# Issuing four scatter DMAs ahead of a bias addition on GpSimd in two of the sixteen blocks of a cross-attention and mixture-of-experts kernel

## The reference

```python
x = x + _L0_xattn_ref(_layernorm(x), ctx_1024, Wq, bq, Wk, bk, Wv, bv, Wo, bo)
x = x + _L0_ffn_ref(_layernorm(x), W_experts, b_experts, W_router, b_router)

# inside _L0_ffn_ref, shortened
router_weights = softmax(einsum('bsd,ed->bse', x, W_router) + b_router)
topk_w, topk_idx = top_k(router_weights, 2)        # all other weights become 0
expert_out = einsum('bsd,eod->bseo', x, W_experts) + b_experts
return einsum('bseo,bse->bso', expert_out, router_weights)
```

## Time and profile before

| | |
|---|---|
| median of 3 runs | 1247.7 us (1247.05 to 1251.27) |
| the profiled execution | 1251.27 us; its span 1249.6 us |
| TensorE busy | 1173.5 us, 94% of the span |
| VectorE, ScalarE, GpSimd busy | 869.7, 712.5, 762.5 us (70, 57, 61%) |
| mean granted TensorE clock | 0.977 |

### The profile page before, as it was taken

The page is one execution under the profiler, slowest core; times in us unless marked ns, Lnnn a source line. Parts: engine busy times, 40 slices in busy tenths (PEclk is TensorE's granted clock), DMA queues, the critical chain, the costliest instruction groups (busy, mean ns, idle before and its releaser), DMA issues. The chain is left out here.

```text
span 1249.6 us, 35422 instructions
## 1 busy us (share of the span) xinstructions
PE 1173.5 (94%) x10864; PEld 708.9 (57%) x10865; DVE 869.7 (70%) x1931; ACT 712.5 (57%) x1040; POOL 762.5 (61%) x996
## 2 busy tenths in 40 slices
PE   7977999999999999999999988799999999999995
PEld 4454666666666666666666655444545555455552
DVE  3665798899889889988987886555545555455553
ACT  4327757866976886696687557243333334333432
POOL 5004347777877877787787678765554545445444
PEclk9978999999999999999999998799999999999998
DMA  9764445755866675586557548889999999988885
GB/s 243 225 180 123 130 139 162 227 183 179 256 185 204 197 224 188 184 253 185 200 178 204 168 148 339 305 189 202 204 184 184 191 183 177 179 168 160 156 165 106
DMA packets 136312, 239.18 MB, mean 191 GB/s; under 512 B 19463, under 2 KB 50183, under 8 KB 135047
## 3 DMA queue, kind: packets, MB, share of 16 engines
q1 hardware_dynamic: 103271, 161.24, 43.6%
q0 software_dynamic: 29808, 67.73, 26.7%
q10 hardware_dynamic: 3120, 8.68, 2.0%
HBM read 112.00 MB, written 101.40 MB: 171 GB/s over the span
## 5 line engine op out<-in xcount | busy, mean ns | idle before, releaser
L1904 PE MATMUL S<-we_s,wq_s 128*128 x1620 | 371.8, 379 | 11.7 <-DVE att L1882 8.3
L1832 POOL DMA_INDIRECT out<-xn,to x135 | 208.9, 1547 | 198.6 <-DMA out<-xn,to 90.1
L1904 PEld LDWEIGHTS S<-we_s,wq_s 128*128 128x128 f16 x1620 | 156.6, 98 | 177.3 <-issue 16.2
L1166 POOL TENSOR_TENSOR we_s<-P_s,we_s 128x1024 f16<-128x1024 f32 x96 | 204.7, 2135 | 72.8 <-ACT we_s L932 71.6
L1843 ACT ACTIVATE wq_s<-PVp 128x512 f16<-128x512 f32 x137 | 81.6, 597 | 249.7 <-PE PVp L1894 249.7
L980 DVE TENSOR_REDUCE mx_sb<-S 128x6 f32<-128x924 f32 x160 | 171.1, 1110 | 10.5 <-PE S L726 8.9
L746 PE MATMUL W<-wo_s,aT_hi 128*128 128x512 f16 x512 | 165.3, 385 | 2.7 <-DVE aT_lo L958 1.4
L708 PE MATMUL W<-we_s,wq_s 128*128 128x512 f16 x512 | 160.9, 386 | 3.7 <-DVE xnT_lo L958 3.6
L1882 DVE SCALAR_TENSOR_TENSOR att<-S,be_s 128x512 f32<-128x512 f32 x135 | 93.4, 692 | 98.8 <-PE S L1904 98.2
L1262 POOL DMA_INDIRECT dispatched<-xn,idx x112 | 114.9, 1026 | 26.7 <-issue 24.0
L1860 DVE TENSOR_TENSOR wq_s<-PVp,wq_s 128x512 f16<-128x512 f32 x137 | 94.6, 691 | 35.1 <-ACT wq_s L1843 35.1
(11 more groups left out here) (204 smaller groups left out, 1948.3 us busy)
## 6 DMA issues: line engine op xcount, KB each, us to landing
P_s<-dispatched SPq DMA_DIRECT2D x139, 260.5 KB, 3.8
we_s<-we_s SPq DMA_DIRECT2D x186, 128.0 KB
be_s<-in_x SPq DMA_DIRECT2D x16, 1024.0 KB, 8.9
xR_s<-in_x SPq DMA_DIRECT2D x16, 1024.0 KB, 8.2
out<-xR_s SPq DMA_DIRECT2D x16, 1024.0 KB, 5.9
wst<-in_weT SPq DMA_DIRECT2D x16, 512.0 KB, 5.7
we_scratch<-wsp SPq DMA_DIRECT2D x16, 512.0 KB, 9.2
Kst<-k_scratch SPq DMA_DIRECT2D x16, 480.0 KB, 9.0
```

The lines of the kernel that those rows point to most:

```text
L1166: e.tensor_tensor(Pst[1][:, r:r + 2, :], exps(n), Pst[0][:, r:r + 2, :], ALU.subtract).then_inc(pldp, 1)
L1832: e.indirect_dma_start(out, bass.IndirectOffsetOnAxis(ap=to[u][:, :], axis=0), yw[u % YW], None, bounds_check=N - 1, oob_is_err=False, com ...
L1904: m = e.matmul(Yp[:, u % 2, :], gT[u % 2][xp][:, k, :], we_s[:, bass.ds(n * WN + (wp * KC + k) * D, D)], start=(c == 0), stop=(c == 11))
```

## The change

In `pool_slot` the call of `pool_SC(e, bm1)` now stands before `pool_BX(e, b, 3)`; it stood behind it. The condition is unchanged (`early1` is true for blocks up to 11 and in the loop, so `pool_SC` is issued only for `bm1` = 12 and 13).

```diff
         if early1:
             pool_S1(e, bm1, 1)
+        elif on_bm1 and bm1.here(NB - 3):
+            pool_SC(e, bm1)
         if on_b:
             pool_BX(e, b, 3)
         if early1:
             pool_S1(e, bm1, 2)
-        elif on_bm1 and bm1.here(NB - 3):
-            pool_SC(e, bm1)
```

## The result

| | before | after |
|---|---|---|
| median, us | 1247.75 (7 runs, 1247.05 to 1252.38) | 1257.72 (7 runs, 1250.99 to 1262.6) |
| profiled execution, us | 1251.27 | 1254.19 |
| its span, us | 1249.6 | 1252.4 |
| first expert tile, us from the start | 809.84 | 813.20 |

The change makes the kernel slower: the ratio is 1.0058 with a 95% interval of 1.0037 to 1.0080, which is +7.2 us. The medians lie 10.0 us apart. The ratio is smaller because it also takes in seven further runs of the changed kernel, 1254.94 to 1256.96 us: the mean of its 14 runs is 1256.4 us, that of the kernel before 1249.1 us. The forecast was +3.6 us, 1251.3 us, with a range up to 1254.3; the median of 1257.7 us lies above the range, and so does the mean.

What follows compares the result with a forecast made beforehand. TensorE is busy 377.15 of 399 us in the second stage; the change can only shift its start, through GpSimd's order in block 14's slot. 0 + 4.5 - 0.9 = +3.6 us on 1247.7: 1251.3 us, range 1248.3 to 1254.3.

Steps and rivals of the forecast that it cites:

- The path: From GpSimd in block 14's slot to the first expert tile: L992 4.5 us late, L1019 and tile 3.6 us late.
- the hand-over to the first scatter: Block 14's slot, ScalarE's L620 to GpSimd: the first scatter starts 0.23 us behind L620's end, at 779.78.
- the 0.9 us at L597: Block 14's slot: L597 no longer waits for the scatters, so 0.9 us of the delay is won back.
- Block 13's slot: The addition is ready 0.4 us before L992 needs it, covered by VectorE's row of maxima; cost 0.
- First rival: At the kernel's end, waits set by earlier DMA traffic absorb up to half of 3.6 us, say 1249 us; chance 0.13.
- none of the four forecasts: The forecast shift of 2.5 to 4.6 us (chance 0.68), absorbed (0.13), larger (0.14) and faster (0.05).
- Second rival: TensorE's clock returns one group later in block 15's projection, adding 2.6 us: +6.2, 1253.9 us; chance 0.14.
- Third rival: On GpSimd the addition runs beside the scatters, L992 is not late, 0.9 us gained, 1246.8 us; chance 0.05.

Runs made afterwards that it cites:

- e10: Kernel before with only block 13's four scatters ahead of block 14's addition, block 13's slot as before; chip 5: 1.0036 of the kernel before.
- e9: Kernel before with only block 12's four scatters ahead of block 13's addition, block 14's slot as before; chip 5: 1.0003 of the kernel before.
- e11: Kernel before with the fourth of block 13's first scatters moved behind the norm in block 14's slot; chip 5: 0.9996 of the kernel before.
- e2: Kernel before with only block 12's four scatters ahead of block 13's addition, block 14's slot as before; chip 7: 0.9994 of the kernel before.
- e18: Kernel before with loads of experts 3 to 7 cut to a sixteenth and the experts' index at most 2; chip 10: 0.9989 of the kernel before.
- e1: The changed kernel again, no edit; chip 7: 0.9987 of the kernel before.
- e3: Kernel before with only block 13's four scatters ahead of block 14's addition, block 13's slot as before; chip 7: 0.9988 of the kernel before.
- e14: Changed kernel with 22 matmuls that nothing reads in TensorE's pause ahead of block 14's L847; chip 4: 0.9997 of the kernel before.
- e16: The changed kernel again, no edit; chip 4: 0.9981 of the kernel before.
- e4: Kernel before with the fourth of block 13's first scatters moved behind the norm in block 14's slot; chip 7: 1.0001 of the kernel before.
- e17: The kernel before again, no edit; chip 10: 1.0006 of the kernel before.
- e5: The kernel before again, no edit; chip 2: 0.9994 of the kernel before.
- e8: The changed kernel again, no edit; chip 2: 1.0043 of the kernel before.
- e7: Changed kernel with loads of experts 3 to 7 cut to a sixteenth and the experts' index at most 2; chip 2: 1.0037 of the kernel before.
- e12: Kernel before, GpSimd's order untouched, with 12 unread statistics instructions on VectorE ahead of block 14's L992 for group 3; chip 5: 1.0037 of the kernel before.
- e13: Changed kernel with two of block 14's slot's four scatters ahead of the addition and two behind; chip 4: 0.9972 of the kernel before.

## Why the prediction failed

**The path: right.** L1248 late, L992, the norm, L597, L1195, L1019, block 15's projection, the first tile: each of them moved, in this order, and the times forecast for the first profile (addition 784.73, L992 786.11, L597 789.35, L1019 792.7, tile 813.4) stand within 0.21 us of what it shows (784.55, 785.92, 789.14, 792.52, 813.20). Part of that is luck: the execution was 0.81 us early, and a term was too small by about as much.

**The step that failed: the hand-over to the first scatter, a term of the sum that was too small by 0.7 us.** The working took 0.23 us from ScalarE to GpSimd, from a tensor instruction. The first scatter started 779.65 - 778.74 = 0.91 us behind L620. In the earlier trace rows the scatter had 0.16 us ahead of it, but it could have begun 1.2 us earlier for ScalarE's part (L620 ended at 779.55), and what it needs before its start could pass beside the addition; that this is the reason is argued, and only the two times are measured. With 0.91 in its place the sum is 0.91 + 4.87 + 0.03 + 1.27 + 0.10 = 7.18 us from L620's end to L992, as measured, and L992 is 5.14 us late, not 4.5. Less the 0.9 us at L597 it is +4.2 us, the ruler's number. That alone would have given 1251.9 us, inside the range. e10 shows the same hand-over on chip 5: L620 ends at 777.74, the scatter starts at 778.66.

**Block 13's slot, 0: right.** L992 stays behind L985 here, with the addition done 1.27 us before it (the working had 0.6 us), and e9 measures 1.0003.

**The 0.9 us at L597: right.** L597 starts 0.22 us behind L582; e11 has the gain alone, 0.7 to 0.9 us.

**First rival, absorbed.** Not on the chips on which the kernel takes 1247 us: from the first tile to the end of the span it is 439.8 us before and 439.2 after. On chips 4 and 7 nothing is lost, but not by what the rival named. In three of the four traces of the slower chips that leave L992 early and have no fillers, the same stretch has extra waits that those with the late L992 don't have: e2 and e18 lose 4.7 us to them and read 26.2 on the ruler, where e1, e3, e14 and e16 read 25.7 to 25.8; e4 loses 3.6; e17 loses nothing. It is a case that none of the four forecasts held; the first trace has no such gap.

**Second rival, the clock.** Half-speed groups come in kernels of either order: 6.7 us in the first trace of before and in e5, with no such pause, and 4.56 us in e10 and e16 behind it. **Third rival, scatters beside the engine.** Disproved: the addition starts 0.03 us behind the end of the fourth scatter's row, and L992 waits for it. The four rows hold the engine up to their right edge. The Trainium skill, page "Perfetto Trace Analysis", section "DMA Instruction — SWDGE (GPSIMD)", puts the right edge at the point where the descriptors have been made, not where the data have moved; it doesn't say whether GpSimd's next instruction can start before that point. In this trace it doesn't.

**What put the time above the range stays open.** The first measurement says 7.2 us, of which the hand-over explains 0.6 over the forecast's 3.6. The four later kernels with a late L992 on chips of the same level say 0.36 to 0.43% (e8, e10, e7, e12), 4.5 to 5.4 us, and 4.2 us, 0.34%, lies within the interval of each, though not within the first one (from 1.0037). The first pair's profiled executions differ by 2.9 us. About 3 of the 7.2 us have no place in any trace here.

One rival is untested: the record doesn't name the chip of the first pair. The kernel before has the level of chips 2 and 5 (1247.85, 1247.11), but the changed kernel's mean of 1256.4 us is nearer to its medians on chips 7 and 4 (1255.73, 1254.56) than to that on chip 2 (1253.43). Were its runs made on another chip than those of before, the surplus would be the chip's. The profiled execution doesn't look like it: its ruler starts at 780.74 us (that of before at 781.55), against 778.2 to 780.4 us on chips 2 and 5 and 782.8 to 786.6 on 4, 7 and 10. The range was too narrow upward: it took the change's mechanism for certain and left little for runs of one kernel that spread over 12 us (1250.99 to 1262.6). On the spread alone I can't say more.

## What to carry to other kernels

An instruction that only needs an old input, like a bias addition, belongs ahead of DMAs that wait for something fresh: behind them it inherits their wait, which here made VectorE's next step 5 us late. Price a hand-over with the kind of instruction that receives it, and from a row in which it really waited. A cost of 0.3% has to be measured on a second chip before it is believed: this one shows on chips 2 and 5 and not on chips 4 and 7.

## What the runs showed of the hardware

- The first indirect DMA of GpSimd that waits for another engine starts 0.91 to 0.92 us behind that engine's end (after, e1, e3, e7, e8, e10, e13, e14, e16; chips 2, 4, 5, 7 and that of the first pair), a small tensor instruction 0.22 us (after). If the wait is over by then, it starts 0.16 us behind an addition (before); each following one has a row of 0.96 us with 0.30 us between.
- The same kernel takes 1247 to 1248 us on chips 2 and 5 and 1256 to 1257.5 us on 4, 7 and 10. The traces of the latter in which L992 is early have 0.5-us gaps between small matmuls, with nothing named that they wait for. Together with single waits of 2.7 to 4.8 us on VectorE and ScalarE that the profile calls "remote", they go with up to 4.7 of the 9.5 us (e2, e18). Most of the rest lies earlier: the ruler's start, the end of block 14's projection, comes at 778.2 to 780.4 us in the eight traces of chips 2 and 5 and at 782.8 to 786.6 us in the ten of the slower chips. What delays it was not looked for.
- The first 12 output-projection matmuls in block 15 take from 2.9 us (e10, with a granted clock of 1.00 over that time) to 5.4 us (after, 0.50). Two traces of the changed kernel with no difference in the code, after and e16, differ by these 2 us in the time to the second group, 6.70 and 4.56 us.
